# An attention and mixture-of-experts layer: expert weight rows of 8 KB moved in packets of 4 KB

## What is computed

```
x = x + attention(layernorm(x))      # keys and values: 512 context rows and 512 own rows of the batch
n = layernorm(x)
scores = softmax(n @ gate_w.T)       # 64 experts, the best 6 of each token, at most 128 rows an expert
for each expert e:                   # gx: the up to 128 token rows that chose it
    g, u = split(gx @ gate_up[e])    # 512 -> 2 x 192
    routed[rows of e] += (silu(g) * u) @ down[e] * weight
x = x + routed + silu(n @ sg.T) * (n @ su.T) @ sd.T      # a shared expert for all tokens
```

## Time and profile before

| what | value |
|---|---|
| median of 3 runs | 825.71 us (825.69 to 830.84) |
| the profiled execution: its time | 825.93 us |
| its span, first to last instruction | 824.2 us |
| PE, DVE, ACT, POOL busy | 94%, 72%, 55%, 38% of the span |
| moved by DMA | 180.34 MB in 50676 packets, mean 219 GB/s |
| q1 (SP) / q0 (POOL): share of the 16 DMA engines | 44.2% / 23.5% |

### The profile page before, as it was taken

How to read it: one execution, slowest core, us unless ns; L and a number is a source line. 1 busy time by engine, 2 the same in 40 slices (tenths; PEclk the granted TensorE clock), 3 DMA queues, 4 the chain that set the end, 5 groups by cost and what they waited for, 6 DMA issues and landing times.

```text
span 824.2 us, 10919 instructions
## 1 busy us (share of the span) xinstructions
PE 771.6 (94%) x3886; PEld 655.5 (80%) x3886; DVE 591.1 (72%) x1168; ACT 455.0 (55%) x801; POOL 311.7 (38%) x258
## 2 busy tenths in 40 slices
PE   6999999999999999999998999998999989878982
PEld 5888878888788887888877887897978878767871
DVE  6537576675587665863696998998988989876820
ACT  3433333442334313342345898998888989766720
POOL 1001010455005640156105455555665655655523
PEclk9999999999999999999999999999999999998997
DMA  4962153332712326202746999999999999999778
GB/s 162 319 230 86 71 217 138 104 103 73 275 61 103 107 111 243 103 30 87 288 180 186 350 330 344 324 345 360 307 336 345 341 334 331 342 321 321 153 128 162
DMA packets 50676, 180.34 MB, mean 219 GB/s; under 512 B 7664, under 2 KB 8048, under 8 KB 37872
## 3 DMA queue, kind: packets, MB, share of 16 engines
q1 hardware_dynamic: 31120, 137.64, 44.2%
q0 software_dynamic: 19504, 42.02, 23.5%
HBM read 143.33 MB, written 44.97 MB: 228 GB/s over the span
## 4 chain that ended last, share of the span: by engine, by line
PE 44%; POOL 15%; issue 15%; DMA 11%; DVE 8%; ACT 4%; SPq 1%; POOLq 0%; DVEq 0%; ACTq 0%
PE bank L1097 8%; PE bank L1099 8%; PE bank L1098 7%; POOL xg L1324 5%; POOL out_rows L1332 5%; POOL second_sum L1332 4%; DMA stage<-wvT_in 3%; PE scores L1097 3%; PE scores L1099 3%; PE scores L1098 3%; DMA out_rows<-eo,idx_all 3%; PE bank L905 2%; DMA second_sum<-eo,idx_all 2%; DMA out_rows<-product,idx_all 2%; PE bank L1076 1%
## 5 line engine op out<-in xcount | busy, mean ns | idle before, releaser
L1456 DVE TENSOR_TENSOR gu_lo<-raw,gu_hi 128x768 fp32r<-128x768 f32 x128 | 122.3, 957 | 30.9 <-ACT gu_hi L1376 26.1
L421 POOL DMA_INDIRECT table<-rows,slot x72 | 80.5, 1119 | 157.7 <-DVEq L832 114.1
L1376 ACT ACTIVATE gu_hi<-raw 128x768 fp32r<-128x768 f32 x128 | 107.2, 840 | 11.7 <-DMA raw<-expert_in 11.7
L1097 PE MATMUL ps_gu<-gu_hi,xgT_hi 128*128 128x384 f32 x256 | 94.2, 368 | 1.3 <-DVE xgT_lo L1456 1.3
L1324 POOL DMA_INDIRECT xg<-x_rows,idx_all x64 | 71.6, 1118 | 60.8 <-DVEq L668 27.0
L1099 PE MATMUL ps_gu<-gu_hi,xgT_lo 128*128 128x384 f32 x256 | 88.7, 346 | 0.0
L1098 PE MATMUL ps_gu<-gu_lo,xgT_hi 128*128 128x384 f32 x256 | 88.7, 346 | 0.0
L449 ACT ACTIVATE qT<-bank 128x512 fp32r<-128x512 f32 x32 | 19.2, 599 | 113.1 <-PE bank L1099 104.2
L454 ACT ACTIVATE pbuf<-scores,negmax 128x1024 f32<-128x1024 f32 x16 | 17.9, 1117 | 69.0 <-DVE negmax L603 69.0
L581 DVE TENSOR_TENSOR qT<-bank,qT 128x512 fp32r<-128x512 f32 x32 | 22.1, 689 | 45.6 <-ACT qT L449 36.8
L1097 PEld LDWEIGHTS ps_gu<-gu_hi,xgT_hi 128*128 128x128 f32 x256 | 50.3, 196 | 1.8 <-DVE xgT_lo L1456 1.7
(11 more groups left out here) (273 smaller groups left out, 2224.7 us busy)
## 6 DMA issues: line engine op xcount, KB each, us to landing
raw<-expert_in SPq DMA_DIRECT2D x64, 1024.0 KB
rest<-rest_in SPq DMA_DIRECT2D x32, 256.0 KB
x_rows<-pbuf SPq DMA_DIRECT2D x17, 256.0 KB, 2.1
stage<-wkT_in SPq DMA_DIRECT2D x4, 1024.0 KB
stage<-ctxT_in SPq DMA_DIRECT2D x4, 1024.0 KB
stage<-wvT_in SPq DMA_DIRECT2D x4, 1024.0 KB
stage<-ctx_in SPq DMA_DIRECT2D x4, 1024.0 KB
stage<-woT_in SPq DMA_DIRECT2D x4, 1024.0 KB
```

What stands on the lines that cost most here:

```text
L421: pool.indirect_dma_start(out=table, out_offset=bass.IndirectOffsetOnAxis(ap=slot[:, i, k:k + 1], axis=0), in_=rows[:, i, k, :], in_offset ...
L1097: pe.matmul(out, still[0], moving[0], start=first, stop=False)
L1376: act.activation(gu[n % GU_SLOTS][0][part], gate_up_of(n, part), ACT.Copy).then_inc(weights_high, 1)
L1456: return dve.tensor_tensor(lo, x, hi.bitcast(F32), ALU.subtract)
```

## The change

The DMA that loads an expert's rows gets a largest length of 4096 bytes for its last dimension. Each row of 8 KB becomes two pieces of 4 KB, so the access pattern of the issued instruction is 128 x 2 x 1024 in place of 128 x 2048. Bytes, buffers, semaphores and the order of all instructions stay as they are; so do the 2 KB rows of `rest` and every other DMA.

```diff
@@ -1267,7 +1267,7 @@
     def load_weights(sp, n):
         if n >= RAW:
             sp.wait_ge(weights_split, PIECE_NO["dn", n - RAW, 0] + 1)
-        sp.dma_start(raw[n % RAW][:, :], t["expert"][n]).then_inc(raw_loaded[n % RAW], 16)
+        sp.dma_start(raw[n % RAW][:, :], t["expert"][n], max_dma_last_dim=4096).then_inc(raw_loaded[n % RAW], 16)
         if n % 2 == 0:
             if n >= 4:
                 sp.wait_ge(weights_split, PIECE_NO["dn", n - 3, 0] + 1)
```

## The result

The changed kernel takes 815.84 us (median of 4 runs, 815.23 to 815.89), the kernel before 826.9 us beside it (4 runs, 825.69 to 830.84). The ratio is 0.985 with a 95% interval of 0.9815 to 0.9885: 1.5% faster. The runs were spread over several chips, on which the medians of the kernel before lie between 826.9 and 830.5 us, so small differences between medians of different chips say little.

What follows compares the result with a forecast made beforehand. The prediction took full DMA engines in the expert stage as the bound, with late additions as its form. From 825.93 us, +4.6 (cut rows), -1.9 (overlap) and -0.6 (turns) gave 828.0 us, with an 8-in-10 range of 819 to 838.

Steps and rivals of the forecast that it cites:

- The bound: Expert stage: DMA engines full at share 1.04, late additions only its form; stage ends when the engines' work is done.
- Price of a cut row: Expert weight loads: each of 512 rows an engine costs 9 ns more when cut in two, +4.6 us.
- Overlap: Expert stage: new packet boundaries beside the other queue's packets overlap, 7.3 ns each, half of them counted, -1.9 us.
- Turns: Expert stage: additions land about 1.3 us sooner, weights up to 3.8 us later; only time of engines not full won, -0.6 us.
- the faster rival: Expert stage: additions are the true bound, shorter turns remove ACT's waits and half of PE's idle time; 815 us, chance 0.12.
- The slower rival: Expert stage: cut rows cost 28 ns more and weights come late for ACT at line 1376; 838 us, chance 0.17.

Runs made afterwards that it cites:

- experiment 5: Odd experts' weight loads from 7 on issued by ACT into a second queue, against a one-queue control: 826.51 against 814.11 us at 4 KB, 836.8 against 829.7 at 8 KB.
- 4 KB, control: Changed kernel, all weights in SP's one queue, with ACT also issuing 29 small useless DMAs where the two-queue version issues loads: 814.11 us, ratio 0.9836.
- 4 KB, two queues: Changed kernel with loads of odd experts from 7 on issued by ACT into its own hardware queue, after the first half of gu_hi: 826.51 us, ratio 0.9985.
- experiment 2: Kernel before (8 KB) and changed kernel (4 KB), each without the 76 accumulating DMAs of the chained results: 799.04 and 800.18 us.

## Why the prediction was wrong

*The bound.* The expert stage, the DMA engines as its bound and the additions as the form in which the bound appears were read rightly. The step that failed is the sentence "The stage therefore ends when the DMA engines have done their work, whichever queue gets the turn first". It took the engines' work as fixed, and the share of 1.04 as proof that no DMA time was left to win. But the second queue of weights in experiment 5 leaves bytes and sizes of weight packets as they are, changes the turns, and costs 12.4 us; and the changed kernel moves 2.2% more bytes in the same 240 us (82.83 against 81.07 MB). The single packets of the traces (start, length, queue and size of each) say where the time is, 460 to 700 us, as shares of the 16 engines' 3840 us; packets of one queue and one size are a kind:

| | 8 KB (before) | 4 KB (changed) | 4 KB, control | 4 KB, two queues |
|---|---|---|---|---|
| engine time without any packet, at least | 0.6% | 0.3% | 0.2% | 2.0% |
| time of packets beyond the median of their kind | 5.7% | 3.3% | 3.2% | 4.1% |
| MB moved | 81.07 | 82.83 | 82.70 | 80.67 |

The engines were full before, as predicted. What the cut removed is for the most part time in which packets ran long: 6% of the 8 KB packets took over 1.2 times their median, 0.7% of the 4 KB ones. What the second queue lost again is for the most part time in which engines stood empty. So how the turns fall decides how much full engines do.

*Price of a cut row.* Taken at +9 ns, +4.6 us. By the medians it is just that: a packet of 8 KB takes 309 ns, two of 4 KB take 2 x 159 = 318. By the means it is less, since the long packets went: 41.0 against 40.8 us a MB, 1.6 ns a row, 0.8 us. So against the mean the term is 3.8 us too high. That the surcharge of four pieces of 2 KB gave the 9 ns is chance: by the medians these take 4 x 84 = 336 ns, 27 more than a whole row. At 2 KB a MB costs 5% more. The estimate by the Trainium skill's page "DMA: Bandwidth & Descriptors" was 3.9 ns a row; the 1.6 ns measured are less than half of it.

*Overlap.* Taken at -1.9 us. An overlap exists, but not for the reason given: a boundary needs no partner from the other queue, since the next packet starts 3 to 4 ns early behind one of the same queue as well. 512 new boundaries x 3.7 ns are 1.9 us. That the number fits is luck: 7.3 ns was a mean over the long overlaps behind additions and the short ones behind all others, and it was halved by an argument that the packets do not bear out. Of the rise of the share from 103.9% to 105.1% about two thirds are such overlaps and one third is empty time that was filled.

*A term that was missing.* I put the time of packets beyond their median at nothing, because I priced only the packets that change, at one fixed price. It fell from 5.7% to 3.3%, 2.4% of some 300 us = 7.2 us, the largest single piece. q0's packets, which nobody touched, take part: a MB of them costs 65.7 us instead of 68.0 (additions 180 ns instead of 185 on average, gathers 162 instead of 169). With the filled empty time (0.37%, 1.1 us) and the additions' median (178 to 176 ns, 0.35%, 1.1 us) against the 4.6 and -1.9 us above, these sums give 4.6 - 1.9 - 7.2 - 1.1 - 1.1 = -6.7 us. They are estimates that carry shares of 240 us over to 300; most of the 10 us is named, and the rest, in the last stretch of the stage, I did not split.

*Turns.* Additions were to land sooner, POOL's waits to fall to 50 to 70 us: the direction was right, the size not (94.2 us; per wait 2.4 to 1.6 us). New waits for raw came, 2.1 us. q1 was to be done a few us later than 773: its last weight packet ends at 761.2 us, against 768.7 before, so the 773 us were too late already for the kernel before. The rule of alternating by packet, which the Trainium skill's page "DMA: Bandwidth & Descriptors" states in "Queues, rings and completion order", agrees with the trace: 108 packets against 111 in 2 us. The page's packet is larger, typically 9 to 17 descriptors; in this trace the turn passes after every single piece, and only so does the size of a piece matter. I had given this rule to the faster rival and then held it to be worthless in full engines. What I did not do was a sum for which I had the rows: with 157 ns a packet of q0 against 333 ns, turns give q0 157 / (157 + 333) = 32% before, and 157 / (157 + 171) = 48% after, against its need of 45%.

*Rivals.* The faster rival had the time (815 us) and the turns right; its reason, that the engines were not the bound, is not borne out, since the share stays at 1.05 and hardly any time without a packet shows in either kernel (at least 0.6% and 0.3%). Its time came from half of PE's 22.0 us of idle time, a half that no row gave, so the hit is in part luck. The slower rival's chain (weights late at line 1376) is what 2 KB packets show, without its price. The rule of "Perfetto Trace Analysis", section "DMA Optimizations" in the Trainium skill, larger transfers when DMA-bound, would have had this change lose; here 8 KB packets lose to 4 KB beside the software queue (826.9 against 815.8 us), and 4 KB win over 2 KB (819.4 us) as the rule says.

*What stays open.* Shown: the gain is lost when the turns are changed back at equal bytes, packet sizes and places of issue (experiment 5), and it is absent where there are no additions and the engines are not full (experiment 2). Also seen in the traces: fewer long packets with 4 KB, and more empty engine time with a second queue. Not shown is what makes a packet run long. The long ones are more frequent where weights are without additions (13% of the 8 KB packets in experiment 2, 6% beside additions), but within the kernel before their mean time does not depend on how many packets of q0 are under way (324 to 335 ns).

## What to carry to other kernels

When two queues share full DMA engines, work out for each the share that turns by packet give it (its packet's time over the sum of one packet of every queue) and compare it with the share it needs. If a queue of small, chained transfers gets less than it needs, cut the other queue's packets until it doesn't, and no further; here, as estimated, 8 KB gave 37%, 4 KB 54%, with 45% needed, and 2 KB paid 5% more for the weights. Spreading the bulk loads over a second queue does the opposite (12.4 us at 4 KB). And do not price a packet by one number: look at how many run long.

## What the runs showed of the hardware that I had not expected

A DMA share of 1.03 to 1.06 went with 329 to 349 GB/s. The part above 1 comes from the record's overlaps: packets of one engine overlap in the record by 3 to 4 ns, behind additions by 20 ns. Weights cost 44.7 us a MB with additions absent and 40.8 beside them. The turn passes between queues after every single piece of a row. And the kernel with 8 KB packets scatters: 821.4 to 833.6 us in 19 runs on one chip, where the changed kernel's eight runs in two sets lie between 812.6 and 815.9 us.
